# Issuing a small on-chip transfer from ScalarE's own queue instead of SyncE's, in a macaron transformer kernel

## The chip, the cores and the metric

One core of one Trainium2 chip runs the whole kernel. The metric is the device time of one execution in microseconds (us), lower is better. The engines are named as in the profile: PE (TensorE, matmuls; PEld are its weight loads), DVE (VectorE), ACT (ScalarE), POOL (GpSimd), SP (SyncE, which here only issues DMA transfers; SPq is its queue). A change is called faster or slower when it moves the time by more than 0.2%, which is about what a measurement of this kernel can tell from no change.

## The reference

The input is 8 sequences of 512 tokens with 128 features. A feed-forward block (`ffn`), a dilated attention block and the same feed-forward block again are applied, with residual additions:

```python
x = x + 0.5 * ffn(layernorm(x))
x = x + attn(layernorm(x))         # dilated: softmax over 16 steps of a 64-token segment, element by element
x = x + 0.5 * ffn(layernorm(x))

def ffn(x):                        # per sequence: 512 tokens x 128
    x = conv1d(x, 3 taps) + conv_b
    q, k, v = split(x @ wqkv.T + bqkv)            # 16 heads of 8
    scores = q @ k.T / sqrt(8)                    # 16 x 512 x 512
    ctx = softmax(scores) @ v
    x = layernorm(x + ctx @ wo.T + bo) * ln1_g + ln1_b
    probs = softmax(x @ gate_w + gate_b)          # 8 experts, all of them used
    h = relu(x @ w1[e] + b1[e])                   # 128 -> 512 for each expert
    y = h @ w2[e] + b2[e]                         # 512 -> 128
    x = layernorm(x + sum_e probs[e] * y) * ln2_g + ln2_b
```

## The kernel before

**Units and ticks.** One unit is one feed-forward block on one sequence: 16 units (`UNITS`), numbers 0 to 7 for the first block and 8 to 15 for the second. A unit is spread over several loop iterations of 64 ticks each; `walk` calls, for every engine, the same list of steps at the tick `T` that the table `AT` gives them, the oldest unit first. So in one iteration the engines work on the scores of unit u, the experts of unit u-2 (and, from tick 48 on, of unit u-1), and the convolution and projections of unit u+1. The order on each engine's queue is fixed by hand in this way, and semaphores tie the engines together. An engine runs its own queue strictly in order.

**A step of two ticks on PE.** At each even tick PE computes one block of the first expert layer (three matmuls L1013, L1014, L1017 into `hid_ps`, from `x1h`, `x1l` and the two parts of `w1`), one of the second layer three blocks behind (L1013, L1014, L1017 from `hidh`, `hidl` and `w2`), two score matmuls for the row maxima (L1056) and two for the probabilities (L1076). At every fourth tick, an odd one, it also computes probabilities times values (L1208, eight matmuls into `ctx_ps`). Other matmuls (convolution L1105 to L1109, projections, transposes) come at their own ticks.

**What ACT evicts.** `hid_ps` is a single PSUM bank. ACT writes the block's ReLU out of it: for an even block number twice, as `hidh` (L737) and as `hid` (L740), for an odd one only `hid` (L740; DVE then casts it, L838). PE starts the next block's matmuls only when `hid` of this block is written (the wait on `h_full`). Toward the end of the last two units (`alone`) the blocks alternate between two banks and this wait reaches one block further back. Between the evictions ACT computes the exponentials of the scores, `probs` (L711; in the first units in halves, L704 and L707).

**The row maxima.** The softmax needs the maximum of each row of scores before the exponentials. The scores are computed twice: first for the maxima, which DVE reduces (L881) to `negmax`; then for the probabilities, where the negated maxima enter through extra rows 94 to 97 of the packed queries `Qp`. For each of four groups g of a unit, at ticks 19, 35, 51 and 67 (`NM_AT`; 67 is tick 3 of the next iteration), POOL splits the maxima into two parts `nm_parts`, PE transposes them (L1141) into PSUM bank `misc`, ACT copies them to the SBUF tile `m_rows` (L687, 32 partitions x 128), and a DMA transfer brings `m_rows` (16 KB) into the four rows of `Qp` for two pairs of heads. PE waits for its landing (`a_m_in`) before the first probability scores of the group, five ticks later (`ready_for_probs`). ACT's next copy into `m_rows` also waits for it.

**The queue of SP.** SP issues this transfer (L469) at the tick behind the copy, after a wait on `a_mr`, the semaphore that the copy raises. It issues all the other transfers of the loop too, in the order of their ticks, among them the loads of the packed queries and keys from DRAM (L461), the gates (L475, L484), and activations in and out. ACT issues no transfers. At tick 36, right behind the transposed maxima of tick 35, PE does the convolution of the next unit.

Of the kernel before, what the change touches and what calls it, by code (L numbers as in the profile page):

```python
# [10 lines left out]
F32 = mybir.dt.float32  # L11
# [23 lines left out]
MAX_ROW, MAX_ROWS = 94, 4  # L35
# [14 lines left out]
RING = 4  # L50
GATE_RING = 4
MID_FIRST = 3
CLOCK_FILL = {k: 12 if k == 14 else 1 if k % 2 == 0 else 0 for k in range(14, 56)}
SECOND_LOAD_AT = -27
BUSY = (20, 5, 5)
# [32 lines left out]
def wait(eng, sem, value):  # L88

    if isinstance(value, int) and value <= 0:  # L90
        return
    eng.wait_ge(sem, value)


def macaron(nc, x, Wq, bq, Wk, bk, Wv, bv, Wo, bo, conv_w, conv_b, wqkv, bqkv, wo, bo2, ln1_g, ln1_b,
            gate_w, gate_b, w1, b1, w2, b2, ln2_g, ln2_b, out):
    with ExitStack() as ctx:
        def sb(name, shape, dt=F32):
            return ctx.enter_context(nc.sbuf_tensor(name, shape, dt))
# [45 lines left out]
        Qp, Kp = sb("Qp", [128, PAIRS, S], F32R), sb("Kp", [128, PAIRS, S], F32R)  # L145
# [4 lines left out]
        m_rows = sb("m_rows", [2 * HG * TC, 128])  # L150
# [46 lines left out]
        s = {}  # L197
# [31 lines left out]
        def chunks(tile):  # L229
            return tile[:].rearrange("p (c d) -> p c d", c=TC)  # L230
# [9 lines left out]
        NM_AT = {19 + 16 * g: g for g in range(G)}  # L240
# [9 lines left out]
                             for n in range(UNITS)]  # L250
                            + [(TICKS * n + at, g, n, NM_FREE[g]) for at, g in NM_AT.items() for n in range(UNITS)]
                            + [(TICKS * (b + MID_FIRST) + AT[op], op, b, free) for op, free in MID_FREE.items()
                               for b in range(B)], key=lambda use: use[0])
# [3 lines left out]
        def in_iteration(i0, back):  # L257
            if isinstance(back, tuple):
                return MID_FIRST <= i0 - back[1] < MID_FIRST + B
            return 0 <= i0 - back <= LAST_UNIT  # L260
# [12 lines left out]
        def walk(i, parity, i0, unit_tick, mid_tick=None):  # L273


            for t in (h / 2 if h % 2 else h // 2 for h in range(2 * TICKS)):
                for back in (0, -1):
                    if mid_tick and in_iteration(i0, ("mid", back)):
                        mid_tick(t + TICKS * back, Unit(i - back - MID_FIRST, parity), t, i, i0)
                for back in (2, 1, 0, -1):  # L280
# [94 lines left out]
        def chunks_of(n):  # L375

            return LOAD_CHUNKS if n else FIRST_CHUNKS
# [17 lines left out]
        def _(sp):  # L395
# [38 lines left out]
            def wait_sp(sem, value):  # L434

                wait(sp, sem, value)
                sp.sem_inc(s["held_sp"], 1)
# [5 lines left out]
            def tick(T, u, t, i, i0):  # L443

                for k, at in ((0, u.at["f_qs"]), (1, u.at["f_ks"])):
                    if T == at:
                        for use in s["pack_in"]:
                            for chunk_in in use:
                                wait_sp(chunk_in, u.count(CHUNK_LOADS, 0))
                        for part, written in enumerate(("f_p1", "f_p2")):  # L450
                            wait_sp(s[written], u.count(2, k + 1))
                            for run in RUNS[k][part]:
                                sp.dma_start(dram[k][run].rearrange("d h q -> h d q"),
                                             parts[k][:, part, :].bitcast(F32)).then_inc(s["parts_out"][k], 16)
                if T in LOADS_AT:
                    k, use, chunk = (LOADS_AT if u.n else FIRST_LOADS_AT)[T]
                    lo, hi = chunks_of(u.n)[use][chunk]
                    wait_sp(s["parts_out"][k], u.count(48, 48))
                    wait_sp(s[("a_s1", "a_s2")[use]], (u.n - 1) * 32 + TC * hi)
                    for half, at in enumerate(DATA_AT[use]):  # L460
                        sp.dma_start((Qp, Kp)[k][at:at + PRODUCT_ROWS, lo:hi, :].bitcast(F32)  # L461
                                     .rearrange("p i q -> p (i q)"),
                                     dram[k][:, :, PAIRS * half + lo:PAIRS * half + hi, :]
                                     .rearrange("a d i q -> (a d) (i q)")).then_inc(s["pack_in"][use][chunk], 16)

                if T - 1 in NM_AT:
                    g = NM_AT[T - 1]
                    wait_sp(s["a_mr"], u.count(4, g + 1))
                    sp.dma_start(Qp[MAX_ROW:MAX_ROW + MAX_ROWS, 2 * g:2 * g + 2, :].bitcast(F32), m_rows[:])\  # L469
                        .then_inc(s["a_m_in"], 16)  # L470

                if T == u.at["gate_out"]:
                    wait_sp(s["c_prTs"], u.count(1, 1))
                    wait_sp(s["y_gated"], u.count(8, 0))
                    sp.dma_start(gate_dram.rearrange("e (c t) -> c e t", c=TC), gateT).then_inc(s["gate_out"], 16)  # L475
                for e in range(E):
                    if T == (u.at["gate_in"] if e < GATE_RING else u.at["experts"] + DOWN_LAG + 7 + 8 * (e - GATE_RING)):
                        if e == 0:
                            wait_sp(s["gate_out"], u.count(16, 16))
                            if i0 < 2:  # L480
                                sp.wait_ge(s["set_wl"], 2 * E)
                        if e >= GATE_RING:
                            wait_sp(s["y_gated"], u.count(8, e - GATE_RING + 1))
                        sp.dma_start(gate_b128[:, e % GATE_RING, :], gate_dram[e].partition_broadcast(128))\  # L484
                            .then_inc(s["gate_in"][e % GATE_RING], 16)

                for n in (u.n, 1):
                    if n > 1 and T == u.at["f_load"] or n == 1 and u.n == 0 and T == SECOND_LOAD_AT:
                        wait_sp(s["f_xT"], n)
                        wait_sp(s["m_stored"], (n - B + 1) * 16)  # L490
                        sp.dma_start(chunks(f_xn), stream_in(n)).then_inc(s["f_in"], 16)
                if T == u.at["e_load"]:
                    wait_sp(s["m_stored"], min(u.n, B) * 16)
                    wait_sp(s["e_stored"], (u.n - B) * 16)
                    sp.dma_start(chunks(resid), stream_in(u.n)).then_inc(s["e_in"], 16)
                if T == u.at["e_store"] and u.n >= B:
                    wait_sp(s["e_x"], u.count(1, 1))
                    sp.dma_start(rows_of(out, u.n % B), chunks(resid)).then_inc(s["e_stored"], 16)
# [136 lines left out]
        def _(act):  # L635
# [10 lines left out]
            def tick(T, u, t, i, i0):  # L646
# [7 lines left out]
                if T == u.at["f_xh"]:  # L654
                    wait(act, s["f_xT"], u.count(1, 1))
                    wait(act, s["f_conv"], u.count(1, 0))
                    if in_iteration(i0, ("mid", 0)):
                        wait(act, s["m_v"], i - MID_FIRST + 1)
                    wait(act, s["pads_zero"], 2)
# [23 lines left out]
                if T in NM_AT:  # L683
                    g = NM_AT[T]
                    wait(act, s["a_nmT"], u.count(4, g + 1))
                    wait(act, s["a_m_in"], u.count(16 * G, 16 * g))
                    act.activation(m_rows[:], misc[0:2 * HG * TC, 0:128], ACT.Copy).then_inc(s["a_mr"], 1)  # L687
                if T == u.at["f_vs"]:
                    wait(act, s["f_v"], u.count(1, 1))
                    wait(act, s["zero_v"], 1)  # L690
                    wait(act, s["a_pv"], (u.n - 1) * 16)
                    turned = misc[:].rearrange("p (a o i d) -> p a o i d", o=2, i=2, d=DH)
                    for place in range(2):
                        last = act.activation(V[u.parity][:, :, :, 2 * VC * place:2 * VC * place + DH]
                                              .rearrange("p c (a i) d -> p (c a) i d", i=2),
                                              turned[:, :, place, :, :], ACT.Copy)
                    last.then_inc(s["f_vs"], 1)
# [27 lines left out]
                if T == u.at["prTs"]:  # L725
                    wait(act, s["c_prT"], u.count(1, 1))
                    wait(act, s["gate_out"], u.count(16, 0))
                    wait(act, s["m_x"], min(i - MID_FIRST + 1, B))
                    act.activation(gateT, misc[0:TC * E, 0:128], ACT.Copy).then_inc(s["c_prTs"], 1)
# [13 lines left out]
            def mid(T, b, t, i, i0):  # L743
                if T == AT["m_xh"]:
                    wait(act, s["m_xT"], b.count(1, 1))
                    wait(act, s["f_conv"], b.n + MID_FIRST + 1)
                    act.activation(mxh, misc[:], ACT.Copy).then_inc(s["m_xh"], 1)
# [262 lines left out]
        def _(pe):  # L1010
# [36 lines left out]
            def keep_clock(k):  # L1047

                for _ in range(CLOCK_FILL[k]):
                    pe.matmul(banks_for_max(k)[:, 0, 0:3 * D], cwh[:, 0, :], cwh[:].rearrange("p j o -> p (j o)"),  # L1050
# [39 lines left out]
            def tick(T, u, t, i, i0):  # L1090
# [89 lines left out]
                if 0 <= T < 64 and T % 2 == 0:  # L1180
# [3 lines left out]
                    ready_for_max(u.n, T // 2)  # L1184
                    if 32 * u.n + T // 2 in CLOCK_FILL:
                        keep_clock(32 * u.n + T // 2)
# [100 lines left out]
```

## Time and profile before

| | |
|---|---|
| time, median of 3 runs | 1558.99 us (1558.27 to 1561.27) |
| time of the profiled execution | 1559.22 us |
| its span (first to last instruction) | 1557.5 us |
| PE busy | 1502.6 us, 96% of the span |
| DVE, ACT, POOL busy | 1160.8, 1121.3, 1014.9 us |
| copies into `m_rows` and transfers of it | 64 each |

The profile gives, for one execution, the busy time of each engine. A timeline row is: start in us, duration in us, engine, line of the kernel, operation, output<-input, shapes; in square brackets, if any, how long the engine sat idle before the instruction and what released it. Matmuls are pipelined, so the durations of consecutive ones overlap and the distance between their starts is the better measure. The duration of a DMA issue is the time on the issuing queue, not that of the data. The granted clock is given in parts of full speed: 1.00 is 2.4 GHz, 0.50 is 1.2 GHz.

### The profile page before, as it was taken

What the parts mean: (1) busy time and instruction counts of PE and PEld (TensorE: products, weight loads), DVE (VectorE), ACT (ScalarE), POOL (GpSimd) and SP (SyncE); (2) the same over time, 40 slices, a digit from 0 to 9 for tenths busy, and PEclk for the clock granted to TensorE, in tenths of its full rate; (3) what the DMA queues carried; (4) which work ended last, traced back from release to release, by engine and by line L of the source; (5) the groups of instructions that cost most, each with busy time, mean ns of one, the idle gap of its engine ahead of it and who ended that gap; (6) DMA issues with size and microseconds to landing.
All of it is one profiled execution on the core that took longest, in us unless ns stands there. A gap on an engine that the chain in (4) does not pass through costs nothing.

```text
span 1557.5 us, 26116 instructions
## 1 busy us (share of the span) xinstructions
PE 1502.6 (96%) x8318; PEld 832.5 (53%) x8318; DVE 1160.8 (75%) x1834; ACT 1121.3 (72%) x1636; POOL 1014.9 (65%) x978
## 2 busy tenths in 40 slices
PE   4888999999999999999999999999999999999997
PEld 3433555555555555555555555555555555555476
DVE  3767677878778787777877778777777777767486
ACT  2466777677776777777677777777777777777776
POOL 3521668767686776868767686776757677667343
PEclk7799999999999999999999999999999999999999
DMA  7433333152332514233142331514323251521111
GB/s 177 119 92 86 96 87 85 49 140 53 81 91 56 130 42 105 74 88 91 49 131 61 81 92 45 141 48 116 83 75 98 69 117 43 142 51 36 41 43 33
DMA packets 75309, 130.06 MB, mean 84 GB/s; under 512 B 10613, under 2 KB 39206, under 8 KB 70566
## 3 DMA queue, kind: packets, MB, share of 16 engines
q1 hardware_dynamic: 73894, 124.19, 31.2%
q0 software_dynamic: 1280, 4.20, 1.0%
q8 instruction: 69, 1.13, 0.3%
q14 instruction: 66, 0.54, 0.1%
HBM read 97.42 MB, written 29.62 MB: 82 GB/s over the span
## 4 chain that ended last, share of the span: by engine, by line
PE 84%; DVE 8%; issue 3%; SPq 1%; DMA 1%; ACT 1%; POOL 1%; DVEq 0%; ACTq 0%; POOLq 0%
PE hid_y L1013 16%; PE ctx_ps L1208 14%; PE hid_y L1017 13%; PE hid_y L1014 13%; PE score L1056 12%; DVE negmax L881 3%; PE misc L1013 2%; PE score L1076 1%; PE misc L1148 1%; DVE x1n L349 1%; PE score L1013 1%; PE misc L1105 1%; PE misc L1164 1%; PE misc L1141 1%; PE misc L1014 1%
## 5 line engine op out<-in xcount | busy, mean ns | idle before, releaser
L881 DVE TENSOR_REDUCE negmax<-score 128x2 f32<-128x1024 f32 x484 | 590.5, 1220 | 239.4 <-PE score L1056 239.4
L592 POOL TENSOR_TENSOR hidl<-hid,hidh 128x512 fp32r<-128x512 f32 x456 | 584.4, 1293 | 258.1 <-DVE hidh L838 140.8
L711 ACT ACTIVATE probs<-score 128x1024 f32<-128x1024 f32 x468 | 479.5, 1024 | 108.7 <-PE score L1076 108.5
L740 ACT ACTIVATE hid<-hid_y,cols 128x512 f32<-128x512 f32 x484 | 330.9, 684 | 161.9 <-PE hid_y L1017 154.2
L1208 PE MATMUL ctx_ps<-probs,V 128*18 128x512 f32 x2048 | 271.5, 602 | 3.2 <-DVE ctxT L888 3.2
L1056 PE MATMUL score<-Kp,Qp 24*128 24x512 f32 x968 | 244.9, 500 | 23.8 <-DMA Kp<-k_parts_dram 16.1
L1076 PE MATMUL score<-Qp,Kp 32*128 32x512 f32 (+1 forms) x1024 | 265.9, 499 | 0.0
L1013 PE MATMUL hid_y<-x1h,w1h 128*128 128x512 f32 x484 | 236.2, 488 | 1.5 <-DVE negmax L881 1.3
L369 POOL TENSOR_TENSOR yacc<-yacc,gated 128x512 f32<-128x512 f32 x127 | 170.6, 1343 | 61.8 <-DVE gated L854 61.8
L737 ACT ACTIVATE hidh<-hid_y,cols 128x512 fp32r<-128x512 f32 x256 | 174.7, 682 | 34.4 <-PE hid_y L1017 31.9
L1056 PEld LDWEIGHTS score<-Kp,Qp 24*128 24x128 f32 x968 | 90.5, 183 | 197.4 <-issue 138.2
L1013 PE MATMUL hid_y<-hidh,w2h 128*128 128x512 f32 x484 | 195.7, 404 | 0.0
L1014 PE MATMUL hid_y<-x1h,w1l 128*128 128x512 f32 x484 | 192.1, 397 | 0.0
L1017 PE MATMUL hid_y<-hidl,w2h 128*128 128x512 f32 x484 | 191.9, 397 | 0.0
L1017 PE MATMUL hid_y<-x1l,w1h 128*128 128x512 f32 x484 | 191.1, 395 | 0.0
L1014 PE MATMUL hid_y<-hidh,w2l 128*128 128x512 f32 x484 | 190.2, 393 | 0.0
L1013 PEld LDWEIGHTS hid_y<-x1h,w1h 128*128 128x128 f32 x484 | 91.9, 190 | 153.1 <-ACT hid L740 95.2
L1013 PEld LDWEIGHTS hid_y<-hidh,w2h 128*128 128x128 f32 x484 | 91.1, 188 | 35.7 <-POOL hidl L592 11.9
L1076 PEld LDWEIGHTS score<-Qp,Kp 32*128 32x128 f32 (+1 forms) x1024 | 98.9, 182 | 11.9 <-ACT probs L707 4.6
L1017 PEld LDWEIGHTS hid_y<-x1l,w1h 128*128 128x128 f32 x484 | 91.2, 188 | 22.2
L1017 PEld LDWEIGHTS hid_y<-hidl,w2h 128*128 128x128 f32 x484 | 90.9, 188 | 22.2
L838 DVE CAST hidh<-hid 128x512 fp32r<-128x512 f32 x228 | 102.1, 448 | 0.0
(203 smaller groups left out, 1828.4 us busy)
## 6 DMA issues: line engine op xcount, KB each, us to landing
gate_b<-gate_dram SPq DMA_DIRECT2D x128, 256.0 KB, 3.6
q_parts_dram<-q_parts SPq DMA_DIRECT2D x48, 256.0 KB, 3.0
k_parts_dram<-k_parts SPq DMA_DIRECT2D x48, 256.0 KB, 3.1
Qp<-q_parts_dram SPq DMA_DIRECT2D x64, 192.0 KB
Kp<-k_parts_dram SPq DMA_DIRECT2D x64, 192.0 KB
Qp<-q_parts_dram SPq DMA_DIRECT2D x30, 240.0 KB
Kp<-k_parts_dram SPq DMA_DIRECT2D x30, 240.0 KB
Qp<-q_parts_dram SPq DMA_DIRECT2D x30, 144.0 KB
```

What stands on the lines that cost most here:

```text
L369: eng.tensor_tensor(ya[:], ya[:], gated[:], ALU.add).then_inc(s["y_acc"], 1)
L592: pool.tensor_tensor(hidl[:, n % RING, :], hid[:, n % 2, :], hidh[:, n % RING, :].bitcast(F32), ALU.subtract).then_inc(s["h_lo"], 1)
L711: act.activation(probs[:, n % 2, 2 * j:2 * j + 2, :], score2[:], ACT.Exp, scale=SCALE)\
L737: act.activation(hidh[:, n % RING, :], hid_bank(u, n)[:], ACT.Relu, bias=col(n))\
L740: act.activation(hid[:, n % 2, :], hid_bank(u, n), ACT.Relu, bias=col(n))\
L881: dve.tensor_reduce(negmax[:, g % 2, :, k % 8], banks_for_max(u.count(32, k))[:], AX.X, ALU.max, negate=True).then_inc(s["a_max"], 1)
L1013: pe.matmul(dst, hi, rhi, start=start, stop=False)
L1014: pe.matmul(dst, lo, rhi, start=False, stop=False)
L1017: return pe.matmul(dst, hi, rlo, start=False, stop=stop)
L1056: last = pe.matmul(banks_for_max(32 * n + k)[:, half, :], Qp[first:end, pair, qc * 128:(qc + 1) * 128], Kp[first:end, pair, :], start=True ...
L1076: last = pe.matmul(score2[:, half, :], Kp[first:end, 2 * g + j, kc * 128:(kc + 1) * 128], Qp[first:end, 2 * g + j, :], start=True, stop=True)
L1208: last = pe.matmul(ctx_ps[32 * j:32 * j + 2 * VC, :], V[p][:, kc, HG * half + 2 * bank + pair, VC * place:VC * place + 2 * VC], probs[:, n ...
```

## The change

ACT issues the transfer itself, right behind its copy, for all units (`MAX_BY_ACT` is 99 and there are 16 units); SP no longer issues it and no longer waits for the copy.

```diff
+MAX_BY_ACT = 99
...
@@ block.sync, tick
-                if T - 1 in NM_AT:
+                if T - 1 in NM_AT and u.n >= MAX_BY_ACT:
                     g = NM_AT[T - 1]
                     wait_sp(s["a_mr"], u.count(4, g + 1))
                     sp.dma_start(Qp[MAX_ROW:MAX_ROW + MAX_ROWS, 2 * g:2 * g + 2, :].bitcast(F32), m_rows[:])\
...
@@ block.scalar, tick
                     wait(act, s["a_m_in"], u.count(16 * G, 16 * g))
                     act.activation(m_rows[:], misc[0:2 * HG * TC, 0:128], ACT.Copy).then_inc(s["a_mr"], 1)
+                    if u.n < MAX_BY_ACT:
+                        wait(act, s["a_mr"], u.count(4, g + 1))
+                        act.dma_start(Qp[MAX_ROW:MAX_ROW + MAX_ROWS, 2 * g:2 * g + 2, :].bitcast(F32), m_rows[:])\
+                            .then_inc(s["a_m_in"], 16)
```

## Rows read from the trace of the kernel before

**Rows 1.** The page: busy times by engine, and the chain's shares.
```profile
PE 1502.6 (96%) x8318; PEld 832.5 (53%) x8318; DVE 1160.8 (75%) x1834; ACT 1121.3 (72%) x1636; POOL 1014.9 (65%) x978
...
PE 84%; DVE 8%; issue 3%; SPq 1%; DMA 1%; ACT 1%; POOL 1%; DVEq 0%; ACTq 0%; POOLq 0%
```

**Rows 2.** Waits of PE from 160 to 1550 us: total, times, longest.
```profile
PE ctx_ps L1208 <- DVE ctxT L888: 3.2, 12, 0.7
```

**Rows 3.** Tile m_rows: durations in ns min/median/max, first and last start; then who waited.
```profile
L687 ACT ACTIVATE m_rows<-misc x64: 246/250/266, 45.9 to 1452.7; 32x128 f32<-32x128 f32 x64
L469 SPq DMA_DIRECT2D Qp<-m_rows x64: 631/643/728, 46.2 to 1453.0; - x64
...
  PE score L1056: 4.8, 1
```

**Rows 4.** Timeline around one copy at tick 3 (tick 67 of its unit).
```profile
634.58 0.25 ACT L687 ACTIVATE m_rows<-misc 32x128 f32<-32x128 f32 x1
...
634.74 0.66 ACT L737 ACTIVATE hidh<-hid_y,cols 128x512 fp32r<-128x512 f32 x1
...
634.93 0.67 SPq L469 DMA_DIRECT2D Qp<-m_rows  x1
...
635.31 0.66 ACT L740 ACTIVATE hid<-hid_y,cols 128x512 f32<-128x512 f32 x1
...
635.88 1.00 ACT L711 ACTIVATE probs<-score 128x1024 f32<-128x1024 f32 x1
...
636.49 0.50 PE L1013 MATMUL hid_y<-x1h,w1h 128*128 128x512 f32 x1
...
637.50 0.69 ACT L740 ACTIVATE hid<-hid_y,cols 128x512 f32<-128x512 f32 x1 [0.63 <-PE hid_y L1017]
```

**Rows 5.** Timeline around one copy at tick 51.
```profile
612.82 0.25 ACT L687 ACTIVATE m_rows<-misc 32x128 f32<-32x128 f32 x1
...
613.38 0.69 ACT L737 ACTIVATE hidh<-hid_y,cols 128x512 fp32r<-128x512 f32 x1 [0.31 <-PE hid_y L1017]
...
614.73 0.48 PE L1013 MATMUL hid_y<-x1h,w1h 128*128 128x512 f32 x1
```

**Rows 6.** Convolution matmuls from 160 to 1550 us: count, first and last start.
```profile
L1105 PE MATMUL misc<-xh,cwh x39: 398/399/501, 213.5 to 1321.0; 128*128 128x512 f32 x39
```

**Rows 7.** Timeline behind one copy at tick 35: the copy, the next first-layer block.
```profile
681.29 0.25 ACT L687 ACTIVATE m_rows<-misc 32x128 f32<-32x128 f32 x1
...
685.51 0.50 PE L1013 MATMUL hid_y<-x1h,w1h 128*128 128x512 f32 x1
```

**Rows 8.** Timeline of ACT behind the copy of 127.72 us.
```profile
129.15 0.60 ACT L704 ACTIVATE probs<-score 128x512 f32<-128x512 f32 x1 [1.19 <-PE score L1076]
```

**Rows 9.** Tile Kp: durations of SP's load issues in ns min/median/max.
```profile
L461 SPq DMA_DIRECT2D Kp<-k_parts_dram x128: 289/354/1025, 28.0 to 1391.7; - x128
```

**Rows 10.** Timeline of POOL around a transfer that POOL issues itself.
```profile
51.47 0.81 POOL L527 DMA_DIRECT2D gate_b<-in_L_ffn_w  x1 [0.29 <-POOL w1l L563]
52.31 1.05 POOL L357 TENSOR_TENSOR f_xn<-f_xn,f_ve 128x512 f32<-128x512 f32 x1
```

**Rows 11.** Timeline around the copy of 81.34 us, in unit 0.
```profile
80.24 1.07 SPq L461 DMA_DIRECT2D Kp<-k_parts_dram  x2
...
81.69 0.68 SPq L469 DMA_DIRECT2D Qp<-m_rows  x1
...
88.82 0.79 PE L1056 MATMUL score<-Kp,Qp 24*128 24x512 f32 x2 [4.83 <-DMA Qp<-m_rows]
```

**Rows 12.** Windows: length, busy PE PEld DVE ACT POOL, granted clock, DMA share, GB/s.
```profile
84.00:86.00 2.00, 0.00 (x0) 0.00 (x0) 0.69 (x1) 1.15 (x3) 0.77 (x1) 1.00 0.69 140
...
86.80:93.60 6.80, 4.78 (x25) 2.25 (x25) 2.60 (x3) 2.17 (x4) 0.00 (x0) 0.53 0.51 96
```

**Rows 13.** Timeline of SP: the gates written to DRAM, then read back.
```profile
615.87 0.63 SPq L475 DMA_DIRECT2D gate_dram<-rest  x1
...
617.85 2.01 SPq L484 DMA_DIRECT2D gate_b<-gate_dram  x4
```

## The prediction, on record before the changed kernel ran

> **What bounds the kernel now.** I read the page first. PE is busy for 96% of the span and makes up 84% of the chain that ended last; ACT is at 72% busy and hardly on the chain [rows 1]. The waits of PE come next: in the 1390 us from 160 to 1550 us the largest entry is 3.2 us in twelve pieces [rows 2]. So in the steady part PE has next to no gap, and whatever makes PE wait there for the first time is added to the time in full. The tile view of `m_rows` says who waits for the transfer that is moved: PE, once, for 4.8 us, out of 64 transfers [rows 3]. Sixty-three of the 64 landings are hidden already, by the five ticks between the copy and its use, so they can't be gained.
>
> Then the timeline, at the place of the edit. At 634.58 ACT copies the maxima; 0.16 us later it starts `hidh`, at 635.31 `hid`, at 635.88 the exponentials; SP starts the transfer at 634.93. PE starts the next first-layer block, which waits for `hid`, at 636.49 [rows 4]. `hid` ends at 635.31 + 0.66 = 635.97, so this one wait has 0.52 us to spare. The copy of tick 51 looks different on ACT and equal on PE: ACT sits idle 0.31 us behind the copy and starts `hidh` 0.56 us behind it, and PE starts the next block 1.91 us behind it, as in the other case [rows 4, 5].
>
> **What the change removes.** On SP, 64 waits and 64 issues of 0.64 us [rows 3]. I cost them at nothing: SP's next transfers can go out up to 2 us earlier, none of them is waited for by PE in the steady part [rows 2], and the landing of the maxima is not earlier in the usual case, since SP started 0.35 us behind the start of the copy, 0.10 us behind its end [rows 4], which ACT can't undercut by more than that 0.10 us.
>
> **What it adds to ACT.** Per copy, a wait for the copy's own end and one DMA issue, both ahead of everything behind them on ACT's queue: `hidh`, `hid`, the exponentials, and through `hid` the next matmuls of PE. The copy takes 0.25 us [rows 3]. From its end to the issue I take SP's 0.10 us [rows 4]; POOL, waiting on its own previous instruction, needs 0.29 [rows 10], the upper bound. The trace has no issue from ACT. The nearest row is the same transfer on SP, 0.64 us [rows 3]; the bounds are the shortest load issue on SP, 0.29 us [rows 9], and an issue on POOL, 0.81 us [rows 10]. I take 0.64, because it is the same transfer with the same access patterns. Could it be nothing, with ACT free while the transfer is described? POOL's row speaks against it: its next instruction starts at 52.31, 0.03 us behind the end of the issue at 52.28 [rows 10]. I take 0.03 for that too. Sum: `hidh` can start 0.25 + 0.10 + 0.64 + 0.03 = 1.02 us behind the start of the copy instead of 0.16 (or 0.56 at tick 51): ACT is 0.86 (0.46) us late.
>
> **What of it PE sees.** From the start of `hidh` to that of `hid` are 0.57 us, `hid` takes 0.66 [rows 4]; I add 0.04 us for the semaphore, an estimate from the 0.03 us above. PE can start its block 1.02 + 0.57 + 0.66 + 0.04 = 2.29 us behind the copy. It started at 1.91 in both patterns. So PE stalls 0.38 us, wherever `hidh` and `hid` follow and PE has nothing longer between.
>
> Is something else late too? The exponentials start at 1.02 + 1.14 = 2.16 us behind the copy and end at 3.16 (they were at 1.30 and took 1.00 [rows 4]). The `hid` of the next block was started at 637.50, 2.92 us behind, after 0.63 us of idleness [rows 4]. With PE's block 0.38 us later it is due at 3.30, so ACT has caught up by then and nothing is late a second time. DVE and POOL take `hid` later by about 0.9 us; the product that needs their result is three blocks behind.
>
> **How many times.** Of the 64 copies: six come before the experts run (unit 0's four and unit 1's first two). There ACT has other work or idles: behind the copy of 127.72 us it waited 1.19 us for PE before the next exponentials [rows 8], more than the 0.86. Those of tick 35 have the convolution of the next unit between: PE's next block is at 685.51, 4.22 us behind the copy [rows 7], so 2.29 is hidden. There are 39 / 3 = 13 of these in the steady part [rows 6]. The last copy, at 1452.7, falls where blocks alternate between two banks. That leaves 64 - 6 - 13 - 1 = 44 stalls: 44 x 0.38 = **16.7 us added**.
>
> **What can be gained at the start.** The one visible wait is that of 83.99 to 88.82 us. The transfer was issued at 81.69, 0.4 us behind the end of two loads of `Kp` on the same queue, and was 7.0 us under way [rows 11]. A transfer of the same 16 KB in a quiet stretch takes at most 617.85 - 615.87 = 1.98 us, since SP waits for it before it goes on [rows 13]. The DMA engines were still 69% busy from 84 to 86 us [rows 12]. If the transfer on another queue no longer stands behind those loads, it lands between 83.7 and 88.7, and PE resumes between 84.5 and 88.8, where 84.5 is 83.99 with some 0.5 us of ACT's lateness, an estimate under the 0.86 us above: a gain of 0 to 4.3 us. The idle time was followed by a granted clock of 0.53, the lower level most of the time, from 86.8 to 93.6 us, with PE busy for 4.78 us of it [rows 12]; at 1.00 that work is worth some 2.4 us less. So the bounds are 0 and 6.7 us. I take 3.5, near the middle: the queue is bypassed, but the 16 engines are busy with its loads.
>
> For the size of this term the Trainium skill has a rule: by its page "DMA: Bandwidth & Descriptors", section "Queues, rings and completion order", SP and ACT own separate rings on each of the same DMA engines, and an engine goes round the rings packet by packet. By it the transfer would pass nearly all of the queue, and the whole 6.7 us would be gained; no row here shows two such rings side by side. The same page's section "Issuing engines are not separate DMA queues" says that using several engines only saves the issuer's time; by that alone nothing would be gained.
>
> **Sum.** 1559.22 us of the profiled execution + 16.7 - 3.5 = 1572.4. Its span of 1557.5 and the 1.7 us around it are not touched otherwise. The profiled execution is 0.2 us above the median of the runs, so I forecast **1572.2 us**, 0.85% slower.
>
> **The rivals.**
>
> *The issue costs ACT little, the change is about neutral.* Price: with 0.29 us for the issue [rows 9] PE could start at 1.94, a stall of 0.03 us, 1.3 us in all; with 0.40 it is 0.14, or 6 us, less the 3.5 us at the start. Time 1556 to 1562. For it: SP's issues reach down to 0.29. Against it: they are of simpler patterns, and all 64 of this one took at least 0.63 [rows 3]. Chance 0.13.
>
> *Faster: the start is gained and ACT's issue is free of cost.* One mechanism, at 83.99 us: the transfer passes the loads, PE does not idle and its clock stays up. Worth up to 6.7 us less 1.3, so 1553.8. It decides once the issue and the waits around it together are under some 0.45 us (instead of 0.77), since then the 44 stalls are worth under 3 us. Against it speaks POOL's row, where the next instruction waits for the issue [rows 10]. Chance 0.09.
>
> *Clearly slower than forecast: ACT's own wait and issue are as long as POOL's.* 0.25 + 0.29 + 0.81 + 0.03 = 1.38 instead of 1.02, PE at 2.65, stall 0.74 us, 44 times 32.6 us: 1588 with the start's gain, 1592 without. For it: ACT is, like POOL, an engine that computes. Against it: POOL's transfers are on another kind of queue. Chance 0.16.
>
> *No change at all* would need slack that rows 2 to 5 do not show; 0.02.
>
> The forecast itself, with an issue of 0.55 to 0.75 us and any gain at the start (44 stalls of 0.29 to 0.49 us, 13 to 22 us, less 0 to 6.7), gives 1565 to 1581; chance 0.60.
>
> **Range and chances.** From 1557 to 1587 lie the forecast (0.60), most of the neutral case and of no change (0.12), and the slow rival's part where only one of its two costs is that long (0.08). Outside are the fast rival and the upper half of the slow one. The forecast's own range is 1565 to 1581. Slower by over 0.2% (beyond 1562.1): forecast, slow rival and 0.02 of the neutral one, 0.78. Within: 0.13. Faster (below 1555.9): 0.09.
>
> **What the profile after would show.** A DMA issue on ACT's queue behind each of the 64 copies, about 0.64 us; `hidh` at 1.02 us behind the copy in both patterns; PE's next first-layer block at 2.29 instead of 1.91 us, with a wait of PE on ACT's `hid` of 0.38 us in 44 places, some 17 us; no such wait behind the copies of tick 35; SP's waits on the copy gone, with no effect; between 81 and 94 us a shorter wait of PE for the maxima and less time at the lower clock. By the Trainium skill's page "Perfetto Trace Analysis", section "DMA Instruction — HWDGE (DVE, Sync)", the sequencer holds its place until the descriptors are made; SP's 0.64 us for 32 rows agrees with that reading but can't show it for ACT. The prediction would be wrong if ACT's issue is far from 0.64 us, if the next ACT instruction starts before the issue ends, or if the short stalls bring the lower clock on, which rows 2 and 12 do not exclude.

## The result and the profile after

The changed kernel takes 1579.91 us in the median of 4 runs (1579.33 to 1581.01), the kernel before 1558.63 us (4 runs, 1557.19 to 1561.27). The ratio is 1.0136, with a 95% interval from 1.0119 to 1.0153: 21.3 us slower (18.5 to 23.8 by the interval), inside the range, 7.7 us above the forecast of 1572.2.

The page of the changed kernel, its busy times and the chain's shares, to be read beside [rows 1]:

```profile
span 1577.9 us, 26052 instructions
...
PE 1510.0 (96%) x8318; PEld 834.3 (53%) x8318; DVE 1169.3 (74%) x1834; ACT 1127.7 (71%) x1636; POOL 1012.9 (64%) x978
...
PE 75%; DVE 9%; issue 6%; ACT 5%; ACTq 2%; DMA 1%; SPq 1%; DVEq 0%; POOL 0%
```

No engine's busy share has moved by more than a point; the shares would not show the loss. The chain does: ACT and its queue rose from 1% to 7% of it. The waits of PE from 160 to 1570 us, beside [rows 2], say what for:

```profile
PE hid_y L1018 <- ACT hid L745: 13.1, 42, 0.4
PE ctx_ps L1213 <- DVE ctxT L893: 3.6, 14, 0.7
```

The first entry did not exist before in this stretch. The tile view of `m_rows`, beside [rows 3]:

```profile
L688 ACT ACTIVATE m_rows<-misc x64: 247/249/267, 46.8 to 1473.1; 32x128 f32<-32x128 f32 x64
L691 ACTq DMA_DIRECT2D Qp<-m_rows x64: 636/637/1242, 47.1 to 1473.3; - x64
...
  PE score L1061: 5.4, 2
```

All 64 issues are on ACT's queue now, 0.64 us each. PE waits twice for the landing, 5.4 us in all, where it waited once for 4.8 us. The first copy is 0.9 us later than before and the last 20.4 us: nearly all the time is lost between them, in equal pieces.

The timeline at the copy that answers to [rows 4] (tick 3):

```profile
642.74 0.25 ACT L688 ACTIVATE m_rows<-misc 32x128 f32<-32x128 f32 x1
...
643.02 0.64 ACTq L691 DMA_DIRECT2D Qp<-m_rows  x1
...
643.76 0.69 ACT L742 ACTIVATE hidh<-hid_y,cols 128x512 fp32r<-128x512 f32 x1 [0.77 <-PE hid_y L1022]
...
644.34 0.68 ACT L745 ACTIVATE hid<-hid_y,cols 128x512 f32<-128x512 f32 x1
...
645.07 0.50 PE L1018 MATMUL hid_y<-x1h,w1h 128*128 128x512 f32 x1 [0.35 <-ACT hid L745]
```

`hidh` starts 1.02 us behind the copy (it was 0.16), `hid` ends 2.28 us behind it, and PE's next block starts at 2.33 instead of 1.91. The idle 0.77 us ahead of `hidh` is put down to PE in the brackets, but PE had long finished, since before the change `hidh` could start 0.16 us behind the copy: it is ACT's own wait and issue. Behind the copy at tick 35, where the convolution stands between, beside [rows 7]:

```profile
690.31 0.25 ACT L688 ACTIVATE m_rows<-misc 32x128 f32<-32x128 f32 x1
...
690.59 0.66 ACTq L691 DMA_DIRECT2D Qp<-m_rows  x1
...
694.52 0.50 PE L1018 MATMUL hid_y<-x1h,w1h 128*128 128x512 f32 x1
```

PE's next block is 4.21 us behind the copy there, as before (4.22): nothing is lost. And at the start, beside [rows 11]:

```profile
47.06 1.24 ACTq L691 DMA_DIRECT2D Qp<-m_rows  x1
...
52.00 0.79 PE L1061 MATMUL score<-Kp,Qp 24*128 24x512 f32 x2 [2.06 <-DMA Qp<-m_rows]
...
82.69 0.66 ACTq L691 DMA_DIRECT2D Qp<-m_rows  x1
...
89.29 0.79 PE L1061 MATMUL score<-Kp,Qp 24*128 24x512 f32 x2 [3.37 <-DMA Qp<-m_rows]
```

The wait that the prediction hoped to shorten still ends 6.6 us behind the issue (7.1 before): PE idles for 3.37 us there instead of 4.83. In exchange a new wait, of 2.06 us, stands at 52 us.

### The profile page after: what moved, and what is told of

The parts are those of the page before. It is cut to its first block, busy times and chain, and to the rows that moved or that the text cites. A ratio compares the mean times of both kernels' runs of the same rounds, so it can differ in the third digit from the quotient of the medians.

```text
span 1577.9 us, 26052 instructions
## 1 busy us (share of the span) xinstructions
PE 1510.0 (96%) x8318; PEld 834.3 (53%) x8318; DVE 1169.3 (74%) x1834; ACT 1127.7 (71%) x1636; POOL 1012.9 (64%) x978
## 3 DMA queue, kind: packets, MB, share of 16 engines
q10 hardware_dynamic: 2304, 1.05, 0.3%
## 4 chain that ended last, share of the span: by engine, by line
PE 75%; DVE 9%; issue 6%; ACT 5%; ACTq 2%; DMA 1%; SPq 1%; DVEq 0%; POOL 0%
PE hid_y L1018 15%; PE ctx_ps L1213 12%; PE hid_y L1022 12%; PE hid_y L1019 11%; PE score L1061 10%; DVE negmax L886 3%; ACT hid L745 2%; ACTq L691 2%; PE misc L1018 1%; PE score L1081 1%; PE misc L1153 1%; ACT probs L716 1%; DVE x1n L350 1%; PE score L1018 1%; DVE hidh L843 1%
## 5 line engine op out<-in xcount | busy, mean ns | idle before, releaser
L843 DVE CAST hidh<-hid 128x512 fp32r<-128x512 f32 x228 | 116.2, 509 | 0.0
```

## The experiments

In each, the time it is compared with is that of the kernel before, measured beside it on the same chip.

### ACT waits but does not issue

```diff
                     act.activation(m_rows[:], ...).then_inc(s["a_mr"], 1)
+                    wait(act, s["a_mr"], u.count(4, g + 1))
```

> ACT keeps the wait for its own copy, SP issues the transfer as before. Theory (the issue of 0.64 us ahead of the evictions is what makes PE late): the next eviction starts some 0.3 us behind the start of the copy instead of 0.16, well under the 0.6 us from which PE sees it, so the time is that of before within 0.2%, 1557 to 1561 us. Rival (the own wait is what costs, since it empties ACT's pipeline): most of the 21 us stay, 1570 us or more.

Measured 1560.25 us against 1557.89, ratio 1.0016 (0.9995 to 1.0037): no difference that can be told. `hidh` starts 0.28 us behind the copy at tick 3 instead of 0.16, and PE's next block is at 1.92 us. The wait for its own copy holds ACT for 0.12 us more; alone it is hidden. The rival, by which this wait is what costs, is out.

### ACT issues but does not wait

```diff
+                    wait(act, s["ident_ready"], 2)
+                    wait(act, s["spare"], u.count(16 * G, 16 * g))
+                    act.dma_start(sink, ident[0:2 * HG * TC, :]).then_inc(s["spare"], 16)
```

`sink` is a scratch in DRAM, and both waits are long fulfilled.

> ACT does not wait for its copy but issues a transfer of the same size and shape, of constant data to a scratch in DRAM; SP issues the real one as before. Theory: the issue alone holds ACT for 0.64 us. If it starts only behind the copy, the next eviction is at about 0.9 us and PE is 0.3 us late 44 times, +13 us, 1572 us. If the issue can run beside the copy, the eviction is at about 0.75 us, PE 0.1 to 0.2 us late, +5 to +8 us, 1564 to 1567 us. Rival (the own wait is what costs): 1557 to 1561 us.

Measured 1558.41 us against 1557.89, ratio 1.0001 (0.9992 to 1.0010): the issue costs nothing. Neither number of my theory allowed for that (+13 us, or +5 to +8). The time is the one that the rival named, but its reason, that the wait alone is what costs, is excluded by the kernel above. The timeline shows why:

```profile
704.84 1.02 ACT L717 ACTIVATE probs<-score 128x1024 f32<-128x1024 f32 x1
704.97 0.31 ACTq L693 DMA_DIRECT2D sink_dram<-ident  x1
...
705.75 0.25 ACT L690 ACTIVATE m_rows<-misc 32x128 f32<-32x128 f32 x1
```

The issue stands behind the copy in the program and starts 0.78 us ahead of it, beside the exponentials; 63 of the 64 issues start while an earlier activation computes. So the queue hands an activation over and goes on, and the issue occupies the queue, not the part that computes. My step, that ACT is held for the length of the issue, was not true as such. But this issue took 0.31 us and not 0.64 (it writes to DRAM, not into `Qp`), so the next pair uses the real shape.

### The same wait and the same issue, in both orders

SP issues the real transfer. ACT issues constant data of the same shape into four unused rows of `Qp` (56 to 59):

```diff
+SPARE_ROW = 56
...
+                    wait(act, s["ident_ready"], 2)
+                    wait(act, s["spare"], u.count(16 * G, 16 * g))
+                    act.dma_start(Qp[SPARE_ROW:SPARE_ROW + MAX_ROWS, 2 * g:2 * g + 2, :].bitcast(F32),
+                                  ident[0:2 * HG * TC, :]).then_inc(s["spare"], 16)
+                    wait(act, s["a_mr"], u.count(4, g + 1))
```

That is the first kernel; in the second the last line stands ahead of the other four.

> ACT issues a transfer of the same shape, of constant data into unused rows of the packed queries, behind the copy and then waits for its own copy; SP issues the real one as before. Theory (an issue runs beside the activations already handed over; only a wait for ACT's own result ahead of it exposes it): no stall in the steady part, the time of before within 3 us, 1556 to 1561 us. Rival (a wait and an issue of 0.64 us on the same queue cost their sum in any order): 1575 us or more.

> The same two instructions in the other order: ACT waits for its own copy, then issues the transfer of constant data; SP issues the real one as before. Theory: 44 stalls of PE of 0.44 us as in the changed kernel, +19 us, 1577 us, with a start like that of before. Rival (they cost nothing apart, so nothing together): 1556 to 1561 us.

Issue then wait: 1558.45 us against 1559.36, ratio 0.9997 (0.9977 to 1.0017). Wait then issue: 1580.25 us, ratio 1.0126 (1.0084 to 1.0168). The same instructions differ by 22 us in their order alone. The timeline of the first, at tick 51:

```profile
703.27 0.64 ACTq L693 DMA_DIRECT2D Qp<-ident  x1
...
704.05 0.25 ACT L690 ACTIVATE m_rows<-misc 32x128 f32<-32x128 f32 x1
704.65 0.69 ACT L745 ACTIVATE hidh<-hid_y,cols 128x512 fp32r<-128x512 f32 x1 [0.35 <-ACT m_rows L690]
...
705.97 0.50 PE L1021 MATMUL hid_y<-x1h,w1h 128*128 128x512 f32 x1
```

and of the second:

```profile
714.07 0.25 ACT L690 ACTIVATE m_rows<-misc 32x128 f32<-32x128 f32 x1
714.35 0.64 ACTq L694 DMA_DIRECT2D Qp<-ident  x1
...
715.09 0.69 ACT L745 ACTIVATE hidh<-hid_y,cols 128x512 fp32r<-128x512 f32 x1 [0.77 <-PE hid_y L1025]
...
716.40 0.50 PE L1021 MATMUL hid_y<-x1h,w1h 128*128 128x512 f32 x1 [0.18 <-ACT hid L748]
```

In the first the 0.64 us run before the copy starts. In the second the wait keeps the queue from running ahead, so the issue begins when the copy has ended and ACT has nothing handed over: all of it is exposed, to 0.01 us as in the changed kernel (`hidh` at 1.02 us, PE's next block at 2.33). The loss of the whole kernel, 20.9 us, is near that of the changed one, 21.3, but its interval of 13 to 26 us is too wide to tell the two apart.

### Two issues behind the wait

```diff
                         act.dma_start(Qp[MAX_ROW:MAX_ROW + MAX_ROWS, 2 * g:2 * g + 2, :].bitcast(F32), m_rows[:])\
                             .then_inc(s["a_m_in"], 16)
+                    wait(act, s["ident_ready"], 2)
+                    wait(act, s["spare"], u.count(16 * G, 16 * g))
+                    act.dma_start(Qp[SPARE_ROW:SPARE_ROW + MAX_ROWS, 2 * g:2 * g + 2, :].bitcast(F32),
+                                  ident[0:2 * HG * TC, :]).then_inc(s["spare"], 16)
```

> The changed kernel with a second issue on ACT right behind the first, of constant data and the same shape. Theory (44 places, each exposed by the issue time): another 0.66 us in each, so PE's next block at about 3.0 us behind the copy instead of 2.34, 44 x 0.66 = 29 us more, 1609 us; behind tick 35 still nothing. Rival (the changed kernel's loss is a fixed price of a stall, not of the issue's length): near 1580 us.

Measured 1619.81 us against 1558.93, ratio 1.0390 (1.0374 to 1.0405). PE's waits from 160 us on:

```profile
PE hid_y L1024 <- ACT hid L751: 46.9, 44, 1.5
```

Exactly 44 waits, one behind each of the copies that the prediction counted. PE's next block is at 3.07 us behind the copy, 0.73 us more than with one issue (0.64 for the issue, 0.09 around it): 44 x 0.73 = 32 us of the 40 us by which this kernel is slower than the changed one. The rest lies ahead of these waits: the copy before the first of them starts 9.2 us later than in the changed kernel (159.59 against 150.35 us). Ahead of it lies a long stretch at the lower clock, which the changed kernel has not:

```profile
103.00:130.00 27.00, 27.00 (x105) 9.07 (x104) 16.89 (x25) 13.80 (x27) 3.71 (x6) 0.50 0.14 30
```

PE was busy through all of it at 0.50, the level of 1.2 GHz (the changed kernel has 1.00 from 95 to 120 us), and I put the rest down to it. What brought the stretch on was not tried, and that it belongs to the second issue is not shown. In the steady part the loss grows with the length of the exposed issue; a stall has no fixed price here.

### Only at tick 35

ACT issues only group 1, SP the other three (`if g == 1` on ACT, the opposite on SP).

> ACT issues only the transfer of tick 35 in each unit, where the convolution stands between; SP issues the others. Theory: its 13 cases in the steady part are hidden, no wait of PE on the eviction, 1557 to 1561 us. Rival (any issue on ACT costs its 0.9 us somewhere): 16 x 0.44 = 7 us or more, 1565 us.

Measured 1559.21 us against 1558.93, ratio 0.9997 (0.9977 to 1.0018). `hidh` is as late there as in the changed kernel (1.04 us behind the copy) and PE's next block is still at 4.21 to 4.23 us: the same delay, covered by the convolution. My expectation had no wait of PE on the eviction at all. There is one, of 0.4 us: behind the copy of tick 35 in the last unit, where no convolution of a next unit is left, PE's block comes at 2.36 us.

```profile
PE hid_y L1018 <- ACT hid L745: 0.4, 1, 0.4
```

So it is the convolution that covers, not the tick. The prediction counted 13 covered copies and not 14, and had this one right.

### Behind the evictions

ACT issues one tick later, behind `hidh` and `hid` and ahead of the exponentials, still with its wait. SP has neither the wait nor the issue, as in the changed kernel.

```diff
+                if T - 1 in NM_AT:
+                    g = NM_AT[T - 1]
+                    wait(act, s["a_mr"], u.count(4, g + 1))
+                    act.dma_start(Qp[MAX_ROW:...], m_rows[:]).then_inc(s["a_m_in"], 16)
                 if P2_AT <= T < P2_AT + 64 and (T - P2_AT) % 2 == 0:
```

> ACT issues the transfer one tick later, behind the two evictions of the next block and ahead of the exponentials. Theory (the place on ACT's queue decides): the evictions are not late, the exponentials start some 0.7 us later and have more than 1 us to spare, so the time is that of before within 0.3%, 1556 to 1563 us. Rival (ACT has 64 issues of 0.64 us more to do, 41 us, and anywhere on its queue they cost about the same): 1575 us or more.

Measured 1561.02 us against 1557.89, ratio 1.0019 (1.0005 to 1.0033). PE's next block is at 1.91 us again and no wait on the eviction is left. The exponentials are not late either: at the copy of 658.58 us they start 1.30 us behind it, as before. The copy has ended when the queue reaches the wait, and the issue (659.74 to 660.38) runs beside `hid` and them. A little is left, 3 us by the medians (0.8 to 5.1); the next two kernels look for it at the start.

### The start: with and without SP's wait

ACT issues only unit 0's four transfers (`MAX_BY_ACT = 1`).

> ACT issues only the four transfers of unit 0, SP all the others. It asks what the start yields. My prediction took 3.5 us of gain there, the changed kernel's trace shows PE waiting nearly as long, to 89.3 us. If the trace is right the time is that of before within 2 us, 1557 to 1560 us. If the start did yield the predicted 3.5 us and the stalls in the steady part ate it, 1555 us.

Measured 1562.03 us against 1557.89, ratio 1.0031 (1.0016 to 1.0046): 4.1 us slower, above both expectations. The same with SP keeping its wait for the copy and only leaving out the issue:

```diff
-                if T - 1 in NM_AT and u.n >= MAX_BY_ACT:
+                if T - 1 in NM_AT:
                     g = NM_AT[T - 1]
                     wait_sp(s["a_mr"], u.count(4, g + 1))
-                    sp.dma_start(Qp[MAX_ROW:...], m_rows[:]).then_inc(s["a_m_in"], 16)
+                    if u.n >= MAX_BY_ACT:
+                        sp.dma_start(Qp[MAX_ROW:...], m_rows[:]).then_inc(s["a_m_in"], 16)
```

> As the kernel in which ACT issues only unit 0's four transfers, but SP keeps its wait for each copy. Theory (SP's wait held its next loads back, and without it those loads are under way when the maxima must pass): the loads of the packed queries go out behind the first copy again, at about 48 us instead of 33, PE's wait for the maxima at 52 us is gone, and the time is that of before within 2 us, 1556 to 1560 us. Rival (the transfer is slow because it stands on ACT's queue): the wait at 52 us and the extra 3 to 4 us stay, 1561 to 1563 us.

Measured 1560.19 us against 1559.36, ratio 0.9992 (0.9971 to 1.0014): no difference that can be told, 0.2 us above the theory's 1556 to 1560 and below the rival's 1561. The intervals of the two kernels just exclude each other. PE's waits for the maxima in the first and in the second:

```profile
PE score L1061 <- DMA Qp<-m_rows: 6.4, 2, 3.7
```

```profile
PE score L1062 <- DMA Qp<-m_rows: 4.7, 2, 4.0
```

The new wait at 52 us, 3.67 us long in the first, is not in the second (which has one of 0.75 us at 102.7 us). SP's timeline in the changed kernel and in the second of the two tells the difference, the loads of unit 0's packed queries and keys for the probabilities:

```profile
33.01 0.70 SPq L462 DMA_DIRECT2D Qp<-q_parts_dram  x2
33.90 0.78 SPq L462 DMA_DIRECT2D Kp<-k_parts_dram  x2
```

```profile
45.67 0.75 SPq L462 DMA_DIRECT2D Qp<-q_parts_dram  x2
46.59 0.70 SPq L462 DMA_DIRECT2D Kp<-k_parts_dram  x2
```

Without the wait they go out 13 to 15 us earlier (before, at 47.61). The windows around the first copy, in the kernel before and in the changed one; the last two columns are the DMA engines' share and GB/s:

```profile
46.00:48.00 2.00, 0.65 (x2) 0.14 (x2) 1.86 (x8) 1.18 (x3) 1.60 (x4) 0.50 0.04 12
```

```profile
46.00:48.00 2.00, 1.51 (x5) 0.39 (x3) 1.85 (x10) 0.27 (x1) 1.71 (x3) 0.50 0.76 152
```

Before, the transfer of the maxima met idle DMA engines (0.04); now it meets them 76% busy with loads that nobody needs yet. SP's wait had been the gate that kept them back. The landings in the traces say the same for all kernels: from its issue this first transfer took 4.8 to 6.7 us in the four in which SP lost its wait for it, 2.0 to 2.5 us in eight of the other nine and 3.6 us in the last. The second of these two kernels is among the eight with 2.2 us, and there too the transfer was on ACT's queue: it is not the queue that makes it slow.

### Loads behind the maxima

The kernel before, SP issuing everything. Only unit 1's first loads are moved, from ticks 45 and 48 to 53 and 54 of unit 0, behind the maxima of tick 51.

> The kernel before, SP issuing everything, but the first loads of unit 1 go out behind the maxima of tick 51 instead of ahead of them. Theory (the maxima of unit 0 at 81.7 us are late because these loads fill the DMA engines): PE's wait of 4.8 us and the stretch at the lower clock behind it go, 5 to 7 us less, 1551 to 1553 us. Rival (other transfers, those of POOL's weights and of the parts to DRAM, hold them up, or the later loads are now late for unit 1): 1556 us or more.

Measured 1561.43 us against 1559.36, ratio 1.0008 (0.9988 to 1.0029): no gain. The long wait at 84 us is gone and the next copy starts at 93.44 us instead of 100.27. But that copy's transfer now stands behind the next loads of unit 1's queries and keys, issued at 89.17 and 90.05, and PE waits 2.73 us for it; then a long stretch at the lower clock follows:

```profile
97.00:121.00 24.00, 22.37 (x88) 7.44 (x89) 13.29 (x20) 10.28 (x20) 3.70 (x6) 0.51 0.18 39
```

Granted clock 0.51, the level of 1.2 GHz, for 24 us in which PE was busy for 22.37: by the copy at tick 35 of unit 1 (129.64 us, before 127.72) the gain is more than given back. So these loads are moved as well, from ticks 1 and 2 of unit 1 to 5 and 6, behind the maxima of tick 3:

```diff
+        SECOND_LOADS_AT = {{-19: -11, -16: -10, 1: 5, 2: 6}.get(t, t): v for t, v in LOADS_AT.items()}
...
-                if T in LOADS_AT:
-                    k, use, chunk = (LOADS_AT if u.n else FIRST_LOADS_AT)[T]
+                loads_at = LOADS_AT if u.n > 1 else SECOND_LOADS_AT if u.n else FIRST_LOADS_AT
+                if T in loads_at:
+                    k, use, chunk = loads_at[T]
```

> The kernel before with two pairs of unit 1's loads moved: the first behind the maxima of tick 51, the second behind those of tick 3. Theory (in the previous try the wait of PE only moved to the next transfer of the maxima, and the long stretch at the lower clock came behind that wait): no wait of PE for the maxima, no lower clock between 85 and 120 us, 5 to 7 us less than before, 1551 to 1554 us. Rival (the lower clock comes from the load on PE there, not from the wait, or the loads land late again elsewhere): 1557 us or more.

Measured 1553.09 us against 1558.93, ratio 0.9969 (0.9951 to 0.9986): 5.8 us less, faster than both kernels of this study. PE waits nowhere for the maxima, and the stretch from 80 to 120 us, here and in the kernel before, has the clock at 1.00 instead of 0.91 (a short stretch at the lower level follows it, 0.83 from 120 to 130 us):

```profile
80.00:120.00 40.00, 36.99 (x221) 13.87 (x217) 34.02 (x49) 27.60 (x55) 9.26 (x15) 1.00 0.40 87
```

```profile
80.00:120.00 40.00, 35.17 (x198) 13.00 (x196) 28.13 (x35) 25.69 (x52) 8.11 (x12) 0.91 0.39 84
```

The profiled execution was 2.3 us ahead at its first copy already, which the moved loads can't have caused; between the third copy and the sixth, where they act, it took 40.5 us instead of 46.4.

## Why the prediction was right, and where it was off

**What bounds, and where the change bites.** Right. PE had no gap, and the wait of the first-layer block for `hid` is where ACT's lateness reaches it. PE waits on `hid` behind 42 or more copies in the three kernels that lose 20 us and more, and behind one at most in all others.

**The size of ACT's delay.** Forecast: issue 0.64 us, `hidh` 1.02 us behind the copy. Measured: 0.64, and 1.02 (1.05 in about a third of the cases). Right in number, but one reason for it was wrong. I took it that an issue holds ACT for its length because POOL's next instruction waits for POOL's issue [rows 10]. On ACT it does not: the real-shaped issue alone, even with a wait behind it, costs nothing (0.9997 of the time before). What exposes it is the wait for ACT's own copy ahead of it, which the change needs because the transfer reads what the copy writes. Each of the two is free alone. So the match to 0.01 us is in part luck: it holds because the wait stands where it does. The same reasoning without the wait gave 5 to 13 us for the issue alone, where nothing was measured.

**The stall and the count.** Forecast 44 stalls of 0.38 us, 16.7 us. The count is confirmed: 44 waits with two issues, none behind tick 35 where a convolution follows. The size was short: PE's next block is at 2.33 to 2.37 us, not 2.29, so a stall is 0.44 us on average and 44 x 0.44 = 19.4 us. (The copies agree: the one at 127.72 us starts 0.7 us later than before, the last one 20.4 us, and the 19.7 us between are 0.45 for each stall.) That is 2.7 of the 8.1 us by which the loss was forecast too small, 13.2 us where 21.3 were measured. The missing 0.04 to 0.08 us are many small things: `hid` takes 0.68 us instead of 0.66 and starts 0.58 behind `hidh`, the way to PE takes 0.05, and in a third of the cases the issue takes 0.66.

**No second lateness.** Right: PE's second block behind the copy is as far behind its first as before, and PE's waits on other results grew by 0.4 us at most.

**The start.** This step failed. It was a gain of 0 to 4.3 us and up to 2.4 us more at the lower clock, taken as 3.5; no kernel in which ACT issues this transfer shows a gain. The transfer did not pass the loads by being on another queue: PE could use it 6.6 us behind its issue instead of 7.1. By the landings, the transfer at this place took 5.8 to 7.1 us in the five kernels in which ACT issued it there and 6.5 to 7.4 us in the six with SP's issue and unmoved loads; in quiet stretches it takes 2.0. From the rings that the Trainium skill's page "DMA: Bandwidth & Descriptors" describes in its section "Queues, rings and completion order", one for SP and one for ACT on each engine, served in turns, the prediction had drawn that the transfer would pass nearly all of the queue. That conclusion is not borne out; whether the engines take turns, these traces don't show. The section "Issuing engines are not separate DMA queues" of the same page fits: the transfers of all issuers run on the same engines, and here the time to landing went with what these had in hand.

**SP's waits and issues: "I cost them at nothing".** This is the other failed step, and the more instructive. I looked for who waits for SP's later transfers and found nobody, but not for what the removed wait held back. SP's next loads went out some 14 us earlier in unit 0 and filled the DMA engines ahead of the first transfer of the maxima; the new wait at 52 us is shown to come from that, by the pair of kernels with and without SP's wait.

What the start cost in all is known less well. By whole times, ACT's issue in unit 0 alone lost 4.1 us (2.5 to 7.2), the kernel with the issue behind the evictions, in which SP lost the same waits, 3.1 us (0.8 to 5.1), and the one in which SP keeps its wait nothing that can be told. The profiles give less. By the start of the copy at tick 35 of unit 1, the seven profiled kernels in which SP kept its waits in unit 0 (one of them but for a single group; the two with moved loads not counted) are at 125.2 to 127.7 us, mean 126.4; the three in which it lost them are at 128.3 to 128.8, mean 128.5 (the kernel with two issues, with its long stretch at the lower clock, left out). Of these 2.1 us, 1.5 stand already at the first copy of all (46.2 against 44.7 us on the mean) and at the end of PE's first wait for `Kp` before it, when the early loads had been issued 2.6 us at most and the DMA engines were as busy in the changed kernel as before (0.70 to 0.82 from 32 to 44 us). The early loads are not shown to be their cause; from the first copy on, the two groups differ by 0.6 us.

So of the 8.1 us by which the loss was forecast too small, 2.7 are the size of the stalls and 3.5 the gain at the start that did not come. The remaining 1.9 us fit a start that lost time instead, 2.1 us by the profiles and 3 to 4 by the whole times; but the interval of the loss, 18.5 to 23.8 us, also holds the 19.4 us of the stalls alone, so that this last part is argued and not measured.

**The rivals.** The neutral and the fast one rested on a cheap issue; it was not cheap where it stood, though without the wait ahead it costs nothing. The slow rival, with POOL's costs, was wrong about ACT by 0.36 us for each copy.

## What to carry to other kernels

A DMA issue on ACT's queue was hidden beside the activations already handed over, unless a wait for ACT's own latest result stood ahead of it; then its whole length was exposed to whatever was queued behind. On POOL this was not tried; its row [rows 10] points the other way. If the transfer must read that result, put it one tick later, behind the evictions that PE waits for, where the result is already there when the queue arrives. And when a wait is taken from a transfer queue, ask what it held back: look at the next issues on that queue and at the DMA engines' share where they will now fall.

## What the runs showed that I had not expected

- With no wait ahead of it, an issue on ACT's queue runs ahead of the activation that precedes it in the program, in the steady part by 0.7 to 0.8 us in nearly all cases, while the activation before that one computes.
- The time of an issue depends on where it writes: 0.64 us for 32 rows of 512 B into four partitions of SBUF, 0.31 us for the same source into DRAM.
- The first issue into `Qp` on ACT took 1.21 to 1.24 us in each of the eight kernels that had one. From the second on it took 0.64 to 0.67, but for a single one of 0.98. The first into DRAM took 0.34 instead of 0.31.
- A transfer on a queue of its own did not pass large loads in hand: 6.6 us from issue to use against 7.1 on the shared queue, with the DMA engines 69% to 85% busy.
- A wait of PE of 2.73 us in the start was followed by a granted clock of 0.51 for 24 us, one of 4.83 us by only 6.8 us at that level, and 44 stalls of 0.44 us in the steady part by none; nor did the 44 waits of some 1.1 us with two issues bring it on (clock 1.00 from 160 to 1610 us). Why the first was followed by so long a stretch stays open.
